# One root, one eps addition and one shift for two norms of neighbouring blocks in a graph kernel

## The reference, cut to what matters

```python
def _layernorm(x, axis=-1, eps=1e-05):
    m = jnp.mean(x, axis=axis, keepdims=True)
    v = jnp.var(x, axis=axis, keepdims=True)
    return (x - m) / jnp.sqrt(v + eps)
...
    h = jnp.maximum(_layernorm(x, axis=-1), 0.0)
    x = x + _L0_gnn_ref(h, src, dst, edge_weight, L0_gnn_weight, L0_gnn_b)
    h = jnp.maximum(_layernorm(x, axis=-1), 0.0)
    x = x + _L1_gnn_ref(h, edge_index, edge_attr_128, node_vec1, node_vec1_n2, L1_gnn_z_in, L1_gnn_z_out, ...)
    h = jnp.maximum(_layernorm(x, axis=-1), 0.0)
    x = x + _L2_gnn_ref(h, edge_index, edge_weight, L2_gnn_wq, L2_gnn_bq, ...)
```

## Time and profile before

| what | value |
|---|---|
| median of 3 executions | 6529.8 us (6518.29 to 6548.38) |
| span of the profiled execution | 6606.6 us, mean granted clock 0.868 |
| DVE busy | 3700.6 us (56%) |
| PE busy | 3748.5 us (57%) |
| POOL busy | 3595.2 us (54%) |
| ACT busy | 1475.8 us (22%) |
| first and last gather of the stage (L983) | start at 1499.6 and 3113.2 us |
| z gathers (L993) | 49 pairs, first at 1636.1, last at 3134.0 us |

### The profile page before, as it was taken

How to read it: one execution, slowest core, us unless ns; L and a number is a source line. 1 busy time by engine, 2 the same in 40 slices (tenths; PEclk the granted TensorE clock), 3 DMA queues, 4 the chain that set the end, 5 groups by cost and what they waited for, 6 DMA issues and landing times. The chain is left out here.

```text
span 6606.6 us, 98591 instructions
## 1 busy us (share of the span) xinstructions
PE 3748.5 (57%) x15612; PEld 2748.4 (42%) x15613; DVE 3700.6 (56%) x12722; ACT 1475.8 (22%) x5078; POOL 3595.2 (54%) x4000
## 2 busy tenths in 40 slices
PE   0000020005776776776677777777779667777676
PEld 0000010004555554555455555555559534444443
DVE  5249691006666666666555555555557656555555
ACT  1000000000111111111455455555546301100000
POOL 4640686755655565555444444444437766655554
PEclk9999999998887888888788888878889878888888
DMA  4320224454444444444333333333332233333332
GB/s 119 85 68 0 73 83 89 118 148 120 127 127 123 125 128 124 127 128 111 93 94 94 96 95 95 94 93 94 97 95 86 89 88 94 91 91 90 90 90 72
DMA packets 505174, 651.54 MB, mean 99 GB/s; under 512 B 86113, under 2 KB 381294, under 8 KB 504944
## 3 DMA queue, kind: packets, MB, share of 16 engines
q0 software_dynamic: 150160, 395.04, 20.9%
q1 hardware_dynamic: 354913, 255.45, 14.3%
HBM read 550.09 MB, written 100.06 MB: 98 GB/s over the span
## 5 line engine op out<-in xcount | busy, mean ns | idle before, releaser
L1398 POOL DMA_INDIRECT a_row<-h_rows,a_idx x832 | 789.8, 949 | 944.0 <-PE a_p_s L1504 396.0
L2005 POOL DMA_INDIRECT r_row<-h_rows,r_idx x832 | 798.3, 960 | 528.7 <-PE r_p_s L2046 267.9
L462 POOL DMA_INDIRECT src_records<-rec,pos_slot x784 | 808.2, 1031 | 419.6 <-issue 250.3
L983 POOL DMA_INDIRECT s_row<-h_rows,s_rec x832 | 804.5, 967 | 281.0 <-issue 242.2
L1018 PE MATMUL s_sums<-s_row,s_hotw 128*128 128x256 f32 x1664 | 661.3, 484 | 519.5 <-DVE s_hotw L1203 315.3
L2046 PE MATMUL r_p_s<-r_row,r_hot 128*128 128x272 f32 x1664 | 644.8, 502 | 362.8 <-DVE r_row L2182 171.9
L1481 PE MATMUL a_p_q<-nodes,a_hotT 128*128 x1664 | 665.0, 486 | 314.9 <-DVE a_score L1551 188.9
L1211 DVE TENSOR_TENSOR nodes<-nodes,s_sums 128x385 f32 x832 | 455.5, 548 | 509.1 <-remote 290.8
L1504 PE MATMUL a_p_s<-a_row,a_masked 128*128 128x257 f32 x1664 | 588.7, 439 | 178.1 <-issue 124.3
L2046 PEld LDWEIGHTS r_p_s<-r_row,r_hot 128*128 128x128 f32 x1664 | 353.1, 234 | 678.8 <-issue 296.2
L1551 DVE CUSTOM_DVE_ANT_0 a_prod<-a_p_q,a_row 128x258 f32<-128x258 f32 x832 | 352.7, 424 | 415.9 <-DMA s_rec<-src_records 187.6
(11 more groups left out here) (315 smaller groups left out, 7511.6 us busy)
## 6 DMA issues: line engine op xcount, KB each, us to landing
s_rec<-src_records SPq DMA_DIRECT2D x832, 66.0 KB
a_locs<-dloc_rows SPq DMA_DIRECT2D x208, 256.0 KB
rec<-in_edge_attr SPq DMA_DIRECT2D x98, 448.0 KB
s_row<-h_rows,s_rec POOLq DMA_INDIRECT x832
a_row<-h_rows,a_idx POOLq DMA_INDIRECT x832
r_row<-h_rows,r_idx POOLq DMA_INDIRECT x832
src_records<-rec,pos_slot POOLq DMA_INDIRECT x784
x_rows<-X SPq DMA_DIRECT2D x1, 6272.0 KB
```

What stands on the lines that cost most here:

```text
L462: gp.indirect_dma_start(out=src_records, out_offset=bass.IndirectOffsetOnAxis(ap=pos_slot[:, k:k + 1], axis=0), in_=rec[:, k, :], in_offse ...
L983: gp.indirect_dma_start(out=row[:, k % R, :], out_offset=None, in_=env["h0_rows"], in_offset=bass.IndirectOffsetOnAxis(ap=rec[:, k % R, DS ...
L1398: gp.indirect_dma_start(out=row[:, k, 0:D], out_offset=None, in_=env["h2_rows"], in_offset=bass.IndirectOffsetOnAxis(ap=idx[:, k:k + 1], a ...
L2005: gp.indirect_dma_start(out=row[:, k % R, 0:D], out_offset=None, in_=env["h3_rows"], in_offset=bass.IndirectOffsetOnAxis(ap=idx[:, k:k + 1 ...
```

## The change

The second norm of block q - 1 and the first norm of block q now share one eps addition (128x2), one root (128x2) and one shift (128x2). The steps EPS2, POW2 and SHIFT2 are gone; the shared ones stand where those of the first norm stood (ADD_EPS 15, POW 18, SHIFT 22). The later steps of the second norm move by two tiles. The shared steps run 50 times, the last time for the second norm of the last block alone (`after` in `woven`). The half of `n_mv` that block 0 has no neighbour for is filled with ones once. The shift, before an operation on one tile with two numbers per partition, becomes an operation on two tiles. The shared root waits for its eps addition, the shift before, and both norms on ACT that read its old result.

```diff
-    STAGE, ..., EPS1 = 5, 7, 7, 8, 9, 10, 11, 10, 12, 12, 13, 14, 15
-    Z1, Z2, G1, G2, POW1, SHIFT1, NORM1, H1, X2, STAT2, AVG2, EPS2 = 14, 15, 16, 17, 18, 22, 23, 25, 26, 27, 28, 29
-    POW2, SHIFT2, NORM2, TURN_H, COPY_H, QK, QUERY = 32, 36, 37, 41, 42, 45, 47
-    LOAD_X, STORE, STORE_T = 0, 40, 44
+    STAGE, ..., ADD_EPS = 5, 7, 7, 8, 9, 10, 11, 10, 12, 12, 13, 14, 15
+    Z1, Z2, G1, G2, POW, SHIFT, NORM1, H1, X2, STAT2, AVG2 = 14, 15, 16, 17, 18, 22, 23, 25, 26, 27, 28
+    NORM2, TURN_H, COPY_H, QK, QUERY = 39, 43, 44, 47, 49
+    LOAD_X, STORE, STORE_T = 0, 42, 46
...
-                def root(m):
-                    def step(q, k, first):
-                        own_wait(gp, with_eps[m], q + 1)
-                        if not first:
-                            own_wait(gp, S["h1_ready" if m == 0 else "h2_ready"], q)
-                        nc.gpsimd.tensor_tensor(rstd[:, m, :], vare[:, m, :], half[:], ALU.pow).then_inc(rooted[m], 1)
-                    return step
+                def roots(q, k, first):
+                    own_wait(gp, with_eps, q + 1)
+                    if not first:
+                        own_wait(gp, scaled, q)
+                        own_wait(gp, S["h1_ready"], q)
+                        if not (isinstance(q, int) and q < 2):
+                            own_wait(gp, S["h2_ready"], q - 1)
+                    nc.gpsimd.tensor_tensor(rstd[:], vare[:], half[:], ALU.pow).then_inc(rooted, 1)
...
-                woven(gp, (0, gather), nodes=[(POOL_LEAD + POW2, root(1)), (POOL_LEAD + POW1, root(0)), (POOL_LEAD + Z, gather_z)])
+                woven(gp, (0, gather), nodes=[(POOL_LEAD + POW, roots), (POOL_LEAD + Z, gather_z)], after=(roots,))
...
                 def norm_x1(q, k, first):
-                    ac.wait_ge(scaled[0], q + 1)
+                    ac.wait_ge(scaled, q + 1)
...
                 def norm_x2(q, k, first):
-                    ac.wait_ge(scaled[1], q + 1)
+                    ac.wait_ge(scaled, q + 2)
...
+                nc.vector.memset(mv[:], 1.0).then_inc(S["spread"], 1)
...
-                        nc.vector.tensor_scalar(vare[:, m, :], mv[:, m, 1:2], EPS, None, ALU.add).then_inc(with_eps[m], 1)
+                    nc.vector.tensor_scalar(vare[:], mv[:, :, 1:2], EPS, None, ALU.add).then_inc(with_eps, 1)
...
-                        nc.vector.tensor_scalar(nmr[:, m, :], mv[:, m, 0:1], rstd[:, m, :], -1.0,
-                                                ALU.mult, ALU.mult).then_inc(scaled[m], 1)
+                    nc.vector.scalar_tensor_tensor(out=nmr[:], in0=mv[:, :, 0:1], scalar=-1.0, in1=rstd[:],
+                                                   op0=ALU.mult, op1=ALU.mult).then_inc(scaled, 1)
```

## The result

The changed kernel takes 6651.8 us (median of 4 executions, 6645.0 to 6654.3) against 6528.1 for the kernel before on the same chip: 1.86% slower, the 95% interval of the ratio being 1.0164 to 1.0208. That is +124 us where +43 was forecast. On two other chips the same kernel was 1.79% (1.0141 to 1.0217) and 1.70% (1.0144 to 1.0196) slower. The direction was right, the size was not.

What follows compares the result with a forecast made beforehand. Bound: POOL's long runs stall DVE, which catches up while POOL waits. Mechanism +2.0 + 0.16 - 0.6 = +1.6 us a pass, early passes about 0; taken +0.9 x 48 = +43 on 6529.8, so 6573 us; range 6480 to 6655.

Steps and rivals of the forecast that it cites:

- What the vanished wait does: POOL no longer stops behind the sixth gather, so the shared root begins later: between -0.9 and +2.0 us a pass.
- Run B 2.5 us longer: POOL's unbroken gathers from z on become two z and eight row gathers, ending at 2089.6 instead of 2087.02.
- x1 1.2 us behind the run's end: DVE's step x1 stays put until POOL's lengthened run has ended, so comes 2.5 us later, at 2090.7.
- PE relief up to 0.6: Two h2 transposes and the QK product move later on PE, shortening DVE's wait: 0 to -0.6 us a pass.
- Phase A +0.16: From the shared root through eight gathers to the next z: 14.75 us remain, plus 0.16 for the root's second column.
- The small terms: Shared steps a column wider: root about 0.72 us on POOL, shift 0.21 to 0.41 us on DVE.
- The page against the trace: Skill's rule that two-input DVE shift and POOL gather contend for SBUF would raise the sum; trace rows show no stretching.
- rival 4: The port: the shared shift stops a gather each time, at most 47 us on top, 6620 us; chance 0.03.
- rival 1: The pass gets shorter: DVE is further on, the z wait shrinks, -0.9 us a pass, 6487 us; chance 0.22.
- Rival 2: Nothing nets out: -0.3 to +0.3 us a pass, within 15 us of before, about 6535 us; chance 0.19.
- Rival 3: POOL's runs merge into 20 us of gathers if the z wait vanishes: +115 us, 6645 us; chance 0.06.
- Rival 5: The moved store of x2, caught in SP's standstill, delays x1: +139 us, 6669 us; chance 0.10.

Runs made afterwards that it cites:

- the stop put back: The padded kernel with POOL stopping again behind the sixth row gather, the shared root unmoved: 0.28% above the kernel before.
- the padded kernel: Changed kernel plus 24 empty DVE instructions ahead of the sums by source and 24 ahead of the attention: 1.57% above before on the first chip, 0.89% on the third.
- the merged kernel: Kernel before with the second norm's root right ahead of the first's and its later steps two tiles later, nothing shared: 1.72% above before, +106 us.
- the store put back: The padded kernel with the store of x2 back at its old position 40: 1.60% above the kernel before.
- The layout alone: Kernel before with 104 empty DVE instructions ahead of the sums by source and 24 fewer ahead of the attention: 1.93% above before, +122 us.

## Why the prediction was wrong in size

**The step that failed** stands in its first sentence: "The change touches one stage only, the sums by source, so I read that stage and nothing else." The sum had no term for where the shorter program of DVE lies; it was put at nothing without a reason. That term is 51 us of the 108 measured on the third chip, 29 in the stage and 23 outside it by the profiled executions, and so most of the 65 us that lie between the forecast and the 108. On the other chips its share is not known. The kernel before had shown that there was something to look at: rows of empty instructions on DVE ahead of the attention and the relations, counted 38 and 26, have no other use there.

**The deciding term** was "What the vanished wait does", with 0.9 us a pass taken between 0 and 1.6. Without the layout the change costs 57 us on the third chip, 38 of them in the stage, by 48 passes 0.8 us each; on the first chip it is 66 us in the stage, 1.4 each. Both are inside the forecast's own range. That the longer run costs was right, as the stop put back shows. That 0.8 lies so near to 0.9 is partly luck: the parts, as follows, came out otherwise.

**Run B 2.5 us longer:** 2.43. Right.

**x1 1.2 us behind the run's end:** wrong. It came 1.3 us ahead of it (2173.49 against 2174.77), and DVE stood still one tile later. What ends with the run is the standstill, not a wait of x1; two instructions of the catch-up are done ahead of it. So the shared root stood 17.55 us behind z and not 18.5, against 16.52 before: +1.0 in a pass without a jump back, not +2.0. And in these +1.0 there is PE at 1.2 GHz, which had no term. The jump back comes on top: on the third chip the passes with one have 33.62 us in the mean and those without 32.39, in the padded kernel 32.40 and 32.60.

**PE relief up to 0.6:** DVE's wait for PE is 3.28 us where it was 3.40, so 0.1.

**Phase A +0.16:** 14.97 us against 14.75, +0.22, in the two passes shown. In the mean over the passes from 1700 to 2950 us it does not hold. On the third chip the root of the first norm stands 18.34 us behind z in the kernel before and 17.67 in the padded one, and from it to the next z it takes 13.25 and 14.80 us; on the first chip it is 17.59 and 18.34, then 14.23 and 15.07. So phase A, priced at almost nothing, carries half of the loss on one chip and all of it on the other. Why it grew was not followed further.

**The small terms:** the wider root has 0.722 us, as worked out (0.72). The shared shift has 0.152 us and lies below both of my bounds (0.206 and 0.406): here the operation on two tiles was cheaper than the one on one tile with two numbers per partition. The eps addition has 0.160 instead of 0.145.

**The page against the trace:** the gathers have a median of 953 ns and a longest of 1117, against 954 and 1362 at line 983 before, and the shared shift is shorter than the old one. Had the contention that SBUF — State Buffer (the Trainium skill, Who interferes with whom) describes come in here, gathers or shift would be longer; no row shows it, and rival 4 falls.

**The other rivals.** The z wait stayed at 4.14 us, so rival 1 (a shorter pass) did not come; it had 0.22. Rival 2, that nothing nets out, falls with the padded kernel, 0.89% above before and clear of noise. Rival 3 came in early passes and, alone, in the merged kernel. Rival 5 was half right: x1 did wait for the store (87.2 us in 35 passes, at line 1235), and the store put back brought nothing, because the same standstill covers it. Its price of 139 us, and rival 3's of 115, would both have come near the measured 124 for a wrong reason.

**Two effects that do not add.** The layout alone cost 122 us on the kernel before, the merged run alone 106, and both together 108 to 124. In the stage both end in the same wait, POOL's for the root, which may be one reason; it was not tested. Another part lies outside the stage, where the layout alone cost about 75 us on the second chip, and in the changed kernel 23 on the third.

## What to carry to other kernels

A wait that stops a long-running engine can be what lets the others work; before taking one away, look whether everybody else is idle in the table of stretches while that engine runs, and try shorter runs instead: here a stop every second gather, with the store moved back, made the kernel 1.36% faster than before. A change that adds or removes instructions moves every later loop of that engine: compare the packets of the instruction queue and the gap at each loop's jump back before believing any reading, and pad if they grew.

## What the runs showed of the hardware that I had not expected

A jump back on DVE took 0.3 us or 2.8 to 3.5 us, by nothing but the place of the program: the same loops, shifted by 24 and 48 instructions, showed both, and so did the kernel before when it was shifted. The Trainium skill has it (Runtime: NRT & Kernel Launch, section Instruction fetch mechanics): a taken branch whose target is outside the two blocks of instructions at hand must fetch the block first. The rows agree in kind, with 398 packets of instructions against 73 and one packet in each of the 65 long gaps; what such a fetch costs, about 2.7 us here (3.0 against 0.3), the page does not say.

Towards the end of a run of POOL's indirect gathers of about ten microseconds, DVE and PE come almost to a halt: DVE was busy 0.04 us of 3.40 in the earlier trace rows. DVE went on 1.2 us behind the run's end in the kernel before, 2.2 in the changed one and 1.5 with the store put back. It is not so in every pass: in the one with the jump back DVE added a tile at 2139.67, 0.9 us ahead of the run's end. The runs show that shorter runs avoid part of the loss. What holds the others back was not shown.

With two more gathers in a run, PE catches up at a lower clock. Behind the run of two z and six row gathers in the kernel before the granted clock was 1.00 in the median, behind that of two z and eight row gathers in the changed one 0.50 to 0.53, after PE had stood idle 3.57 us in the pass shown; the products of one tile took 1.65 us instead of 0.93. So a busy time of TensorE that is read from a stretch before a change need not hold for it afterwards.
